# Linear attention on five engines: the value projection moved to the end of the slot, the slot's other steps set in a new order, and the two middle sequences run as a loop

## The reference, cut to what matters

```
x = x + _L0_attn_ref(_layernorm(x), w_attn, w_proj)

def _L0_attn_ref(x, w_attn, w_proj):              # 16 heads of 16
    q, k, v = split(x @ w_attn)
    q = elu(q) + 1;  k = elu(k) + 1
    # for each position t, causal:
    S = S + k_t (outer) v_t;  z = z + k_t
    y_t = (q_t . S) / (q_t . z + 1e-6)
    return y @ w_proj
```

## Time and profile before

| | |
|---|---|
| median of 3 runs | 3246.8 us (3246.23 to 3248.19) |
| the profiled execution: its time, its span | 3246.23 us, 3244.3 us |
| mean granted TensorE clock | 0.986 of full |
| PE busy | 3079.7 us (95%) |
| DVE, ACT, POOL busy | 2342.9, 1729.7, 1614.6 us |
| share of the chain that ended last: PE | 87% |
| linear attention | about 1251 to 1550 us of the span |

### The profile page before, as it was taken

How to read it: one execution, slowest core, us unless ns; L and a number is a source line. 1 busy time by engine, 2 the same in 40 slices (tenths; PEclk the granted TensorE clock), 3 DMA queues, 4 the chain that set the end, 5 groups by cost and what they waited for, 6 DMA issues and landing times.

```text
span 3244.3 us, 99172 instructions
## 1 busy us (share of the span) xinstructions
PE 3079.7 (95%) x35618; PEld 2684.4 (83%) x35618; DVE 2342.9 (72%) x6549; ACT 1729.7 (53%) x4533; POOL 1614.6 (50%) x1874
## 2 busy tenths in 40 slices
PE   5999989999999998999799999999999899999989
PEld 4888878878887887998588887878888788898878
DVE  6888777677776775776677767767777688776776
ACT  4677642266776223665577773226677622454445
POOL 6777730177776002443677772027777544317610
PEclk9999999999999998999899999999999999999999
DMA  4111121021111111000211112111111110100001
GB/s 154 45 41 46 35 79 35 23 62 41 35 38 38 48 32 47 11 11 11 55 41 36 37 40 74 33 49 38 40 36 38 49 39 19 27 0 1 1 14 39
DMA packets 182965, 124.91 MB, mean 39 GB/s; under 512 B 27628, under 2 KB 179528, under 8 KB 182216
## 3 DMA queue, kind: packets, MB, share of 16 engines
q1 hardware_dynamic: 182728, 121.77, 13.8%
HBM read 48.29 MB, written 23.07 MB: 22 GB/s over the span
## 4 chain that ended last, share of the span: by engine, by line
PE 87%; DVE 6%; issue 3%; POOL 1%; ACT 1%; DMA 1%; SPq 0%; DVEq 0%; ACTq 0%; POOLq 0%
PE bank L310 16%; PE bank L311 13%; PE bank L312 13%; PE bank L463 8%; PE bank L432 6%; PE bank L404 3%; PE bank L636 2%; PE bank L635 2%; PE bank L634 2%; PE bank L628 2%; PE bank L629 2%; PE bank L441 2%; PE bank L580 2%; PE bank L579 2%; PE bank L443 2%
## 5 line engine op out<-in xcount | busy, mean ns | idle before, releaser
L2349 POOL TENSOR_TENSOR prob<-prob,rsum 128x384 f32<-128x384 f32 x512 | 415.4, 833 | 158.8 <-DVE rsum L1645 158.8
L1074 ACT ACTIVATE prob<-prob,nmax 128x192 f32<-128x192 f32 x1024 | 456.0, 454 | 2.3 <-DVE nmax L1638 2.2
L1223 ACT ACTIVATE gate<-bank,bias 128x512 f32<-128x512 f32 x192 | 132.2, 689 | 517.6 <-PE bank L312 517.6
L2336 POOL TENSOR_TENSOR rn<-ss,mhalf 128x16 f32<-128x16 f32 x128 | 375.6, 2934 | 10.6
L2317 POOL TENSOR_TENSOR rstd<-meanvar,eps 128x4 f32<-128x4 f32 x48 | 12.3, 256 | 676.3 <-DVE meanvar L1572 676.3
L1638 DVE CUSTOM_DVE_ANT_0 prob<-bank,masks,rn 128x192 f32<-128x192 f32 x768 | 274.5, 414 | 100.2 <-PE bank L432 99.1
L310 PE MATMUL bank<-wqkv_hi,hT_hi 128*128 128x512 f32 x768 | 331.4, 432 | 15.2 <-DVE rot_t L1600 7.2
L2343 POOL TENSOR_TENSOR qk<-rot_t 128x512 f32<-128x512 f32 x256 | 333.0, 1302 | 6.9 <-DVE ss L1612 6.9
L311 PE MATMUL bank<-wqkv_lo,hT_hi 128*128 128x512 f32 x768 | 304.9, 397 | 0.0
L312 PE MATMUL bank<-wqkv_hi,hT_lo 128*128 128x512 f32 x768 | 304.9, 397 | 0.0
L310 PE MATMUL bank<-gT_hi,w_hi 128*128 128x512 f32 x704 | 277.2, 394 | 3.0 <-issue 2.5
(11 more groups left out here) (282 smaller groups left out, 9855.9 us busy)
## 6 DMA issues: line engine op xcount, KB each, us to landing
Vlo<-V SPq DMA_DIRECT2D x256, 64.0 KB, 1.9
Vhi<-V SPq DMA_DIRECT2D x256, 64.0 KB, 2.0
ya<-Y SPq DMA_DIRECT2D x32, 256.0 KB, 2.3
H<-Y SPq DMA_DIRECT2D x128, 64.0 KB, 1.8
H<-ya SPq DMA_DIRECT2D x128, 64.0 KB, 1.8
yb<-Y SPq DMA_DIRECT2D x128, 64.0 KB, 1.6
HB<-Y SPq DMA_DIRECT2D x32, 256.0 KB, 2.8
HB<-yb SPq DMA_DIRECT2D x32, 256.0 KB, 2.9
```

The lines of the kernel that those rows point to most:

```text
L1074: ins = e.activation(pb, pb, ACT.Exp, bias=nm[r][:, x:x + 1], scale=-1.0, accum_out=sums[r][:, x:x + 1])
L2336: e.tensor_tensor(rn[u][:, :], ss[:, :], mhalf[:, :], ALU.pow).then_inc(s_plRN, 1)
L2349: e.tensor_tensor(pair, pair, rs[:, 2 * gi:2 * gi + 2].unsqueeze(2).to_broadcast([P, 2, KW]), ALU.mult).then_inc(s_plPN[gi], 1)
```

## The change

Four things change in the linear attention, and nothing outside it.

1. On PE the order in a slot was q, ty, v, k, pr, ht, sc, num, delta, tr0, yb, tr1. It becomes q, ty, k, ht, pr, sc, num, delta, v, yb, tr0, tr1. ACT and DVE follow: ACT takes ht between rl and ex, and copies state and v after ysum; DVE takes ht before pr.
2. The waits that guard `bank1` go with it: ht waits for the copy of tr1, v for DVE's read of ht, tr1 for the copy of v. The values need two buffers instead of four, and four memsets of the ones column and of the padding each become two.
3. DVE's statistics run a tile further ahead (T+4) and stand around at3 at the end of the slot; POOL's `mg` runs at T+5.
4. Sequences 1 and 2 become a loop over one body of eight slots on PE, ACT, DVE and POOL; sequences 0 and 3 stay unrolled.

```
 # PE, slot
                     if inside(T + 1):
-                        v_(T + 1, (u + 1) % TB)
                         k_(T + 1, (u + 1) % TB)
+                    if inside(T + 2):
+                        ht(T + 2, (u + 2) % TB)
                     if inside(T - 2):
                         pr(T - 2, (u - 2) % TB)
-                    if inside(T + 2):
-                        ht(T + 2, (u + 2) % TB)
 ...
                     if inside(T):
                         delta(T, u)
                     if inside(T + 1):
-                        tr_(T + 1, (u + 1) % TB, 0)
+                        v_(T + 1, (u + 1) % TB)
                     if inside(T - 1):
                         yb_(T - 1, (u - 1) % TB)
                     if inside(T + 1):
+                        tr_(T + 1, (u + 1) % TB, 0)
                         tr_(T + 1, (u + 1) % TB, 1)
 # PE, the guards
 ht: -                    e.wait_ge(z_acV, T + OFF)
     +                    e.wait_ge(z_acTK, T - 1 + OFF)
 v_: -                    e.wait_ge(z_acTK, T + OFF)
     +                    e.wait_ge(z_dvHT, (min(NT, T + 2) if isinstance(T, int) else T + 2) + OFF)
 tr1:-                        e.wait_ge(z_dvHT, ...)
     +                        e.wait_ge(z_acV, T + 1 + OFF)
 # ACT, slot
                     if inside(T + 1):
-                        v_(T + 1, (u + 1) % TB)
                         rl(T + 1, (u + 1) % TB)
-                        ex_(T + 1, (u + 1) % TB)
                     if inside(T + 2):
                         ht(T + 2, (u + 2) % TB)
+                    if inside(T + 1):
+                        ex_(T + 1, (u + 1) % TB)
 ...
                         num(T - 1, (u - 1) % TB)
+                    if inside(T):
+                        state(T, u)
                     if inside(T + 1):
+                        v_(T + 1, (u + 1) % TB)
                         tr_(T + 1, (u + 1) % TB, 0)
                         tr_(T + 1, (u + 1) % TB, 1)
-                    if inside(T):
-                        state(T, u)
 # DVE, slot: ht(T + 2) to before pr; st_, ag_ from T + 3 after ty to
 #   st_(T + 4) before at_(T, u, 3) and ag_(T + 4) after it
 # POOL, slot
-                    if inside(T + 4):
-                        mg(T + 4, (u + 4) % TB)
+                    if inside(T + 5):
+                        mg(T + 5, (u + 5) % TB)
 # PE, ACT, DVE, POOL
-                for b in range(B):
-                    sequence(b)
+                sequence(0)
+                with e.Fori(0, B - 2) as i:
+                    sequence(i + 1)
+                sequence(B - 1)
```

More of the change, by code:

```diff
@@ L205, in build @@
         qkp = [sb(f"qk_pad{i}", [P, 2, H0, 32]) for i in range(2)]
-        va = [sb(f"v_one{i}", [P, H0, 32]) for i in range(4)]
+        va = [sb(f"v_one{i}", [P, H0, 32]) for i in range(2)]
         qT0 = [sb(f"linqT{i}", [P, 4, P]) for i in range(2)]
@@ L707, in linear_attention @@
                 prep['A'] += 2
-                prep['B'] += 12
+                prep['B'] += 8
                 prep['V'] += 2
@@ L717, in ht @@
                     e.wait_ge(z_acXN, T + 1 + OFF)
-                    e.wait_ge(z_acV, T + OFF)
+                    e.wait_ge(z_acTK, T - 1 + OFF)
                     for k in range(KD):
@@ L772, in delta @@
                             o = bank[2][32 * g:32 * g + 32, 32 * c:32 * c + 32]
-                            i = e.matmul(o, qkp[r][:, 1, 4 * c + g, :], va[u % 4][:, 4 * c + g, :], start=u == 0 and c == 0, stop=True, skip_group_check=True)
+                            i = e.matmul(o, qkp[r][:, 1, 4 * c + g, :], va[r][:, 4 * c + g, :], start=u == 0 and c == 0, stop=True, skip_group_check=True)
                     i.then_inc(z_peDL, 1)
@@ L784, in num @@
                             o = bank[3][32 * g:32 * g + 32, c * P:(c + 1) * P]
-                            i = e.matmul(o, va[u % 4][:, 4 * c + g, :], at[r][g][:, c, :], start=c == 0, stop=u == 0, skip_group_check=True)
+                            i = e.matmul(o, va[r][:, 4 * c + g, :], at[r][g][:, c, :], start=c == 0, stop=u == 0, skip_group_check=True)
                     if u > 0:
@@ L1334, in v_ @@
                 def v_(T, u):
+                    r = u % 2
                     e.wait_ge(z_peV, T + 1 + OFF)
-                    e.activation(va[u % 4][:, :, 0:D0], bank[1][:, 0:D].rearrange('p (h d) -> p h d', h=H0), ACT.Copy).then_inc(z_acV, 1)
+                    e.activation(va[r][:, :, 0:D0], bank[1][:, 0:D].rearrange('p (h d) -> p h d', h=H0), ACT.Copy).then_inc(z_acV, 1)
                 def tr_(T, u, j):
@@ L2051, in slot @@
                         ty(T - 2, (u - 2) % TB)
-                    if inside(T + 3):
-                        st_(T + 3, (u + 3) % TB)
-                        ag_(T + 3, (u + 3) % TB)
+                    if inside(T + 2):
+                        ht(T + 2, (u + 2) % TB)
                     if inside(T - 2):
@@ L2071, in slot @@
                         y_(T - 1, (u - 1) % TB)
+                    if inside(T + 4):
+                        st_(T + 4, (u + 4) % TB)
                     if inside(T):
                         at_(T, u, 3)
+                    if inside(T + 4):
+                        ag_(T + 4, (u + 4) % TB)
                 def sequence(b):
@@ L2077, in sequence @@
                         slot(TB * b + u, u)
-                for T in range(-3, 0):
+                for T in range(-4, 0):
                     slot(T, T % TB)
-                for b in range(B):
-                    sequence(b)
+                sequence(0)
+                with e.Fori(0, B - 2) as i:
+                    sequence(i + 1)
+                sequence(B - 1)
                 for T in range(NT, NT + 2):
@@ L2493, in linear_attention @@
                     e.memset(qkp[i][:, :, :, :], 0.0).then_inc(s_prepB, 1)
-                for i in range(4):
                     e.memset(va[i][:, :, D0:VA], 1.0).then_inc(s_prepB, 1)
@@ L2547, in sequence @@
                         slot(TB * b + u, u)
-                for T in range(-4, 0):
+                for T in range(-5, 0):
                     slot(T, T % TB)
-                for b in range(B):
-                    sequence(b)
+                sequence(0)
+                with e.Fori(0, B - 2) as i:
+                    sequence(i + 1)
+                sequence(B - 1)
                 for T in range(NT, NT + 2):
```

11 lines of the change are left out of this document (4 added, 7 removed).

## The result

The changed kernel takes 3269.8 us (median of 4 runs, 3267.65 to 3269.98) against 3246.5 us of the kernel before beside it (4 runs, 3245.54 to 3248.19). The ratio is 1.0069, with a 95% interval of 1.0052 to 1.0087. The forecast was 3265 with 3252 to 3272: slower as expected, by 23.3 us instead of 18.4.

A forecast was written before the change was run, and what follows sets the result against it. It took PE, busy 200.00 of 200 us, to bound the kernel. Two new waits over 29 slots (+20.0), start and end (-1.6) and seams (0) gave +18.4 and 3265 us, range given as 3252 to 3272.

The forecast's parts named there:

- What bounds: Steady linear attention: only work or gaps on PE count; its slack is 0.29 us a slot.
- The q wait: q's first product waits for ACT's copy of tr0, with only tr1 as cover: 0.44 us more a slot.
- The pr wait: pr's first product waits on ty through yT_hi and yT_lo: 1.31 us needed, 1.06 covered, 0.25 a slot.
- The switches: PE's changes between transposes and products: taken as 0, with 0.15 us a slot won or lost as bounds.
- 29 slots: Number of slots, 2 to 30, that pay both waits: 29 x (0.44 + 0.25) = 20.0 us.
- The start: Start of the stage: 0.9 us won by k ahead of v, 0.3 by fewer memsets.
- The end: Slot 31: tr0 stands behind yb, so the y chain starts 0.44 earlier; 0.4 us won.
- The loop's seams: PE's loop entry, jump back and exit: taken as 0, at most 5.4 us at 1.8 each.
- (a): Rival: only q's wait counts, ty's chain being shorter in a full slot; +11.2, 3258 us; 12 in 100.
- (b): Rival: faster, both short gaps on PE filled at the slot's end; -10.0, 3237 us; 8 in 100.
- (c): Rival: no change; switches win 0.15, pr's wait absent, q's wait half; about 0, 3247 us; 5 in 100.
- (d): Rival: PE's clock falls at the new gaps in each slot; three slots at 1.2 GHz, 3289 us; 5 in 100.

The follow-up runs named there:

- E3: E1 with tr0 back ahead of yb on PE; 3252.46 us, ratio 1.0019 to the kernel before, slots of 8.71 us.
- E4: E1 with ht behind pr again on PE, ACT and DVE; 3271.49 us, ratio 1.008 to the kernel before, slots of 9.37 us.
- E9: E1 with ty ahead of q on PE; 3250.83 us against 3245.61 for the kernel before, ratio 1.0021, slots of 8.67 us.
- E1: The changed kernel with all four sequences unrolled on every engine; 3262.88 us, ratio 1.0052 to the kernel before.
- E5: E1 with the loop on PE only; 3270.21 us in one execution, beside 3249.62 for the kernel before; one slot of 14.35 us.
- E6: E1 with the loop on ACT, DVE and POOL but not PE; 3270.31 us in one execution, beside 3249.62 for the kernel before.
- E2: The kernel before with only sequences 1 and 2 made a loop, order unchanged; 3253.04 us, ratio 1.002 to the kernel before.
- E8: The changed kernel, looped, with three quarters of the scores' products left out; one slot of 12.89 us among slots of about 8.88.
- E7: E8 with three quarters of the products also left out of num's state part and delta; 7.90 us across the jump back, neighbours 8.0 to 8.1.

## Why the prediction was right, step by step

- **What bounds.** PE's order and the slack of 0.29 a slot: right. No difference that the order made hung on ACT, DVE or POOL being slower; each lies in what PE has to do between two dependent steps.
- **The q wait, 0.44 a slot.** Right to 0.01: E3 takes exactly it away. The reason to trust it was that the case stood in the trace already, in slot 0.
- **The pr wait, 0.25.** Right: 0.27 on the chain after, 0.22 more where E4 takes away 0.22 of cover, and gone with E9. Read from the one slot without cover.
- **The switches, 0.** Nearly right: the switch behind delta costs 0.20 before v's product instead of 0.15 before a transpose, 0.05 x 29 = 1.5 us.
- **29 slots.** Right; slots 2 to 30 carry it.
- **The start, -1.2.** Right up to the first transposes of tile 0, which come 1.2 earlier behind the start of the stage; PE's wait before them falls from 2.93 to 0.56:

```profile
1265.85 1.97 PE L751 MATMUL bank<-misc,qk_pad 128*128 128x128 f32 x8 [0.56 <-DVE qk_pad L2010]
```

  Slot 0 is another 0.7 shorter, which the forecast did not have: PE's clock is at 0.93 in 1270 to 1272, 3 to 5 us behind the first linqT, where before it was still 0.66 in 1274 to 1276, 2.6 to 4.6 us behind it. The -1.4 of the sum above is these two and +0.44 for slot 1's yb, which now stands ahead of the linqT that serves as the mark.
- **The end, -0.4.** The step was right, its effect was lost elsewhere, and the sum is +0.1. From tr0's end (1547.86, before 1525.42) to the end of pr's first product in slot 31 (1550.18, before 1528.63) it is 2.32 where it was 3.21. Of these 0.89, 0.44 is yb, which now lies ahead of tr0, and 0.45 is the earlier y. ACT's copies of linqT and linkT hold yT_hi up by less than 0.1 (ty ends at 1548.86):

```profile
1547.88 0.60 ACT linqT L1344
1548.48 0.49 ACT linkT L1344
1548.97 0.32 ACT yT_hi L1356
```

  Behind that the stage takes 22.55 where it took 21.58, as the clock falls earlier while the pipeline empties. pr's first product of the next tile on the chain, before and after:

```profile
1536.10 0.38 PE bank L310
```

```profile
1557.65 0.58 PE bank L310
```

  Where the clock falls there differs between kernels that have the same steps at this place: from the last linqT to the end of the stage E1, E5 and E6 take 25.07, 24.85 and 23.93, before 24.75. No such term was in the forecast.

- **The loop's seams, 0.** The failed step, a mis-sized term: 5.4 us in the changed kernel, 4.2 in the profile of E2, 5.2 in E5. Entry and exit cost nothing (their spacings are 9.09 and 9.15); the one jump back costs all of it. The prediction said it would be wrong if PE idled 1 us or more where the body begins again, and on this term it was: it idled 3.38. It took the value of the nearest loop in the trace although that body is shorter. The rule of the Trainium skill (Advanced Engine Details and Errata, ISA Cache), quoted beside it with the count of instructions, spoke against the 0, and the runs bear it out. The bound of 5.4, three landings of 1.8, held the number by luck: there was one stall, larger than one landing, and the clock did the rest.
- **The sum.** +18.4 forecast; by the parts 21.6 + 5.4 - 1.4 + 0.1 = +25.7 in the stage, and +23.3 in the median. The stage's 25.7 on the median before would give 3272.2, just outside the range. That the time is 2.4 less is owed to the rest of the program, which no term of the forecast is about: luck again. The range was also added up too short: with the +4.4 that it names for a switch its upper end is 3265 + 4.4 + 1.6 + 5.4 = 3276.4 and not 3272.
- **Rivals.** (a) fell with E4, where the chain has its full 1.31. (b) and (c) fell with the slot of 9.15. (d), a clock that falls at gaps of 0.57 and 0.27, did not come: it stays at 1.00 over all 9.15-us slots. But it fell for one slot after a gap of 3.4, which (d) had not foreseen.

What stays open: by the medians the order costs 3 us less than by the stage (16.6 against 20.0 in E1), and the loop 2 us more in E2 (6.8 against 4.3). The stages of single executions and medians of totals need not agree at this size, and no run here tells more.

## What to carry to other kernels

When steps on the busiest engine are reordered, write for each dependency that leaves it and comes back what it takes at least (here 1.13 us through ACT, 1.31 through ACT and DVE) and what cover of its own work lies between; the difference is the price per slot, and it is best read from a first or last slot where the cover is missing already. When an unrolled stretch becomes a loop, count the instructions of the body on each engine and weigh them against what the engine holds before taking its seams at nothing. And look for the order in which all dependencies have cover at once: taking one wait away may only uncover the next, as in E9, or may win both.

## What the hardware showed beyond that

- A jump back of a PE loop of 2,240 to 2,624 products and loads leaves PE idle 2.8 to 3.4 us, in the four kernels that have such a loop (the changed one, E2, E5, E8), and in none whose PE program is unrolled. With 1,520 (E7) there is no stall, and no packet of instructions for PE in the second round.
- PE's clock falls to 1.2 GHz behind this one gap and comes back within the slot: in the changed kernel 0.52 of full in 1410 to 1415, 0.80 in the next 5 us, 1.00 after that. So a stall of 3.4 us costs 5.4, and E2's of 2.8 costs 4.2.
- While the pipeline empties, the clock falls at a place that differs from kernel to kernel, and the end of the stage by about 1 us with it.
- Two gaps of under 0.6 us in each slot of 9.15 us leave the clock at 1.00.
- Loops on ACT, DVE and POOL cost nothing that is seen (E6). Their bodies are far shorter, 88, 120 and 80 operations in eight slots, and q14 moves no packet while they loop a second time.
